# Message-passing layer on one core: node table first, radial pieces made inside the message loop, three one-hot buffers

## What is computed

```
s_j   = (silu(x[src][:, 384:] @ W1 + b1)) @ W3 + b3          # depends on the node alone
rbf   = sqrt(2/R) * sin(n * pi * r / R) / r,  n = 1..20      # radial functions of an edge
basis = rbf * cutoff(r) @ W2 + b2                            # 20 -> 384
s1, s2, s3 = split(s_j * basis)
msg   = [ v_j * s1 + s3 * edge_vector , s2 ]
x1    = x + segment_sum(msg, dst)
h     = silu([norm(vUV), s] @ Wu1 + bu1) @ Wu2 + bu2         # of x1, by node; gives a second message by source
x2    = x1 + segment_sum(second message of src, dst)
y     = layernorm(x + x2)
```

## Time and profile before

| | us |
|---|---|
| median of 3 runs | 714.84 (711.1 to 719.67) |
| profiled execution, its span from first to last instruction | 711.8 |
| first gather of the loop (L486) | 144.38 |
| last product of the loop (L929) | 550.55 |
| PE busy in the span | 505.8 (71%) |
| DVE busy | 537.0 (75%) |
| ACT busy | 389.5 (55%) |
| POOL busy | 370.2 (52%) |

### The profile page before, as it was taken

The page is one execution under the profiler, slowest core; times in us unless marked ns, Lnnn a source line. Parts: engine busy times, 40 slices in busy tenths (PEclk is TensorE's granted clock), DMA queues, the critical chain, the costliest instruction groups (busy, mean ns, idle before and its releaser), DMA issues.

```text
span 711.8 us, 13058 instructions
## 1 busy us (share of the span) xinstructions
PE 505.8 (71%) x4260; PEld 234.1 (33%) x4269; DVE 537.0 (75%) x1192; ACT 389.5 (55%) x713; POOL 370.2 (52%) x375
## 2 busy tenths in 40 slices
PE   0276430038888888888888888888888286689996
PEld 0232110013333333334433333333333153344443
DVE  8868861029999999999999999999999443354283
ACT  1054331046777777776776777777776364343200
POOL 5004440067777777777777777777773131025300
PEclk9975555559999999999999999999999688689999
DMA  8413777699888888898888888888884400000021
GB/s 277 166 21 99 199 229 222 183 256 306 269 269 272 269 275 270 267 275 268 269 273 269 270 271 271 270 270 269 273 271 149 160 3 0 1 0 1 2 89 56
DMA packets 54193, 139.26 MB, mean 196 GB/s; under 512 B 10366, under 2 KB 21850, under 8 KB 54124
## 3 DMA queue, kind: packets, MB, share of 16 engines
q0 software_dynamic: 25120, 102.91, 46.3%
q1 hardware_dynamic: 23132, 25.80, 12.8%
q10 hardware_dynamic: 5872, 9.68, 4.1%
HBM read 120.47 MB, written 17.54 MB: 194 GB/s over the span
## 4 chain that ended last, share of the span: by engine, by line
DVE 39%; PE 35%; DMA 8%; issue 8%; ACT 3%; SPq 2%; POOL 2%; DVEq 1%; ACTq 1%; POOLq 0%
PE psum L1192 11%; DVE side L929 10%; PE psum L1282 9%; DVE hot L920 5%; DMA part_rows<-side 5%; DVE side L926 4%; PE psum L1157 4%; DVE work L929 3%; DVE work L947 3%; PE psum L1186 3%; PE psum L1251 3%; DVE hot L911 2%; SPq L358 2%; DVE side L916 2%; DMA side<-node_table,src_c 2%
## 5 line engine op out<-in xcount | busy, mean ns | idle before, releaser
L486 POOL DMA_INDIRECT side<-node_table,src_c x234 | 224.4, 959 | 71.3 <-issue 60.4
L604 ACT ACTIVATE side<-key_no,less_key 128x320 bf16<-128x320 f32 x314 | 159.3, 557 | 30.7 <-SPq L384 28.9
L612 ACT ACTIVATE side<-side,one_f 128x640 bf16<-128x640 bf16 x157 | 128.1, 816 | 10.0 <-PE psum L1168 10.0
L1157 PE MATMUL psum<-w2s,radial 123*128 123x384 bf16 x314 | 78.7, 333 | 66.3 <-DVE side L929 43.5
L1186 PE MATMUL psum<-side,hot 128*32 128x512 f32 x468 | 123.1, 605 | 0.5 <-DVE side L929 0.5
L929 DVE TENSOR_TENSOR side<-side,psum 128x768 f32<-128x768 f32 x117 | 110.5, 945 | 0.0
L486 POOL DMA_INDIRECT work<-node_table,src_c x80 | 76.8, 960 | 60.6 <-SPq L384 36.5
L1192 PE MATMUL psum<-side,hot 128*32 128x128 f32 x1404 | 99.4, 277 | 0.0
L926 DVE TENSOR_TENSOR side<-side,psum 128x512 f32<-128x512 f32 x117 | 79.4, 678 | 1.3 <-DMA side<-node_table,src_c 1.3
L1168 PE MATMUL psum<-side 128*128 128x320 bf16 x314 | 70.3, 306 | 0.5 <-ACT side L612 0.5
L1192 PEld LDWEIGHTS psum<-side,hot 128*32 128x32 f32 x1404 | 68.0, 109 | 0.1
(11 more groups left out here) (202 smaller groups left out, 738.0 us busy)
## 6 DMA issues: line engine op xcount, KB each, us to landing
radial<-part_rows SPq DMA_DIRECT2D x36, 270.0 KB
part_rows<-side SPq DMA_DIRECT2D x6, 810.0 KB, 12.7
side<-node_table,src_c POOLq DMA_INDIRECT x234, 4.2
sum_rows<-stage SPq DMA_DIRECT2D x212, 16.0 KB
node_table<-work ACTq DMA_DIRECT2D x10, 320.0 KB, 7.6
sum_rows<-zeros_bf SPq DMA_DIRECT2D x1, 2688.0 KB, 18.8
side<-sum_rows ACTq DMA_DIRECT2D x10, 256.0 KB, 4.7
xw<-in_x ACTq DMA_DIRECT2D x1, 2304.0 KB
```

The lines of the kernel that those rows point to most:

```text
L486: g.indirect_dma_start(out=rows[i % SLOT_PAIRS][:, j, :], out_offset=None, in_=node_table, in_offset=bass.IndirectOffsetOnAxis(ap=src_c[:, ...
L604: a.activation(key_off[:, b, j, :], key_no[:, :], ACT.Abs, bias=less_key[:, t:t + 1]).then_inc(L["key_off_made"], 1)
L612: a.activation(key_hot[:, b, :, :], key_off[:, b, :, :], ACT.Relu, bias=one_f[:, :], scale=-1.0).then_inc(L["key_hot_made"], 1)
L1157: last = mm(bank[2 * (i % 2) + j][:, 0:C3], radial[0:RROWS + 3, t * P:(t + 1) * P], w2s[:, :], start=True, stop=True)
```

## The change

1. **Node table first.** ACT loads x's s part, W1, b1, W3 and x's vector part into a buffer of their own (`x_in`) ahead of all else, and the zeroing of `sum_rows` goes to its queue. DVE interleaves the ten table multiplies with the edge tables; the table has four buffers (TABLES) and three PSUM banks (FILTER_BANKS), and the multiply reads the filter in PSUM. Casts and edge attribute copies go to ACT, the splits of W2, the constants and the zeroing of the counts to GpSimd.
2. **Radial pieces in the loop.** PIECES is 9, of 768 columns. r and the coefficient are stored as f32 and loaded by broadcast on 120 partitions (`load_r`, `load_coef`), with no pick matrix and no `spread`. Piece 0 is made before the loop, piece i (1 to 8) in it, from pair `piece_at(i)` on, which is 0 for piece 1 and 18(i-1)-8 for the others; its first edges are used at pair 18i. DVE's steps stand behind pairs 0, 1 and 4 of the piece, ACT's (`sine`, `high_part`, `middle_part`) at its steps 3, 5 and 7, GpSimd's two subtractions behind its gathers 13 and 15. `part` and `wave` have one buffer and lie in `xw`; `load_stack` copies from chip memory to chip memory without `part_rows`. SP's steps of a piece (six stack copies, then the rows of the next piece) stand behind the sum store number `stores_before(i)`.
3. **No barrier at the first pass.** The first pass is straight code without `pass_begin`; further passes, if any edge needs them, stand in an `If`. Each engine waits for what it needs itself.
4. **Three one-hot buffers** (HOTS = 3).
5. x is loaded again into `xw` in front of the last three sum stores, and Wu2 goes into W3's tile.

```diff
-HOTS = 2
+HOTS = 3
-PIECES = 6
-PB = 3
+PIECES = 9
+FILTER_BANKS = 3
+TABLES = 4
...
+        def piece_at(i):
+            return 0 if i == 1 else PIECE_PAIRS * (i - 1) - 8
+        def piece_pairs(step):
+            return {piece_at(i) + step: i for i in range(1, PIECES)}
+        def stores_before(i):
+            return -(-(piece_at(i) + 2) // GP)
...
+            def load_r(i):
+                if i:
+                    sp.wait_ge(S["turn_begun"], i)
+                sp.dma_start(r_in, rc_piece(0, i)).then_inc(S["r_loaded"], 16)
+            def load_coef(i):
+                if i:
+                    sp.wait_ge(S["wave_scaled"], i)
+                sp.dma_start(coef_in, rc_piece(1, i)).then_inc(S["coef_loaded"], 16)
             def load_stack(i):
-                sp.wait_ge(parts_stored[i % 2], 16 * (i // 2 + 1))
+                sp.wait_ge(S["lo_made"], i + 1)
                 for q, k in enumerate(STACK):
...
-                                 part_rows[k].rearrange("(n c) f -> n c f", c=CHUNKS)[:, :, i * PC:(i + 1) * PC]
-                                 ).then_inc(stack_in[i], 16)
+                                 part[:, k, :]).then_inc(stack_in[i], 16)
...
+                    if n in pieces:
+                        load_stack(pieces[n])
+                        if pieces[n] + 1 < PIECES:
+                            load_r(pieces[n] + 1)
+                            load_coef(pieces[n] + 1)
+                    if pieces and n == NG - 4:
+                        load_x()
...
+            for b in range(TABLES):
+                pool.wait_ge(table_stored[b], 16 * through(NW, b, TABLES))
...
+            less_high_at, low_at = piece_pairs(SLOT_PAIRS + 5), piece_pairs(SLOT_PAIRS + 7)
+            for i in range(PAIRS):
+                gather(i)
+                if i in less_high_at:
+                    less_high(less_high_at[i])
+                if i in low_at:
+                    low_part(low_at[i])
...
+            def high_part(i):
+                act.wait_ge(S["wave_scaled"], i + 1)
+                if i:
+                    act.wait_ge(stack_in[i - 1], 16 * PARTS)
+                a.copy(part[:, 0, :], wave).then_inc(S["hi_made"], 1)
+            def middle_part(i):
                 act.wait_ge(S["wave_less_hi"], i + 1)
+                a.copy(part[:, 1, :], wave).then_inc(S["mid_made"], 1)
...
+            sine_at, high_at, middle_at = piece_pairs(3), piece_pairs(5), piece_pairs(7)
+            def key_pass(first):
                 for i in range(PAIRS + 1):
                     if i < PAIRS:
                         key_offsets(i)
                     if i:
                         key_hots(i - 1)
+                    if first and i in sine_at:
+                        sine(sine_at[i])
+                    if first and i in high_at:
+                        high_part(high_at[i])
+                    if first and i in middle_at:
+                        middle_part(middle_at[i])
                     if i >= GP + 2 and (i - GP - 2) % GP == 0:
                         take_sums((i - GP - 2) // GP)
...
+            turns_at, remainder_at, scaled_at = piece_pairs(0), piece_pairs(1), piece_pairs(4)
+            def piece_steps(i):
+                if i in turns_at:
+                    turns(turns_at[i])
+                if i in remainder_at:
+                    remainder(remainder_at[i])
+                if i in scaled_at:
+                    scaled(scaled_at[i])
```

More of the change, by code:

```diff
@@ new lines, in _, with gather @@
+            pool.wait_ge(S["edges_turned"], 5)
+            pool.wait_ge(S["span_made"], 2)
+            pool.wait_ge(S["r_stored"], 16)
+            pool.wait_ge(S["coef_stored"], 16)
+            words = NW * TCOL // 2
+            g.memset(work[:, 0:words], 0.0).then_inc(S["counts_zeroed"], 1)
+            def gather(i):
+                if i >= SLOT_PAIRS:
+                    pool.wait_ge(L["summed"], i - SLOT_PAIRS + 1)
+                for j in range(2):
+                    g.indirect_dma_start(
+                        out=rows[i % SLOT_PAIRS][:, j, :], out_offset=None, in_=node_table,
+                        in_offset=bass.IndirectOffsetOnAxis(ap=src_c[:, 2 * i + j:2 * i + j + 1], axis=0)
+                    ).then_inc(gathered[i % SLOT_PAIRS], 16)
@@ L1108, in _ @@
[L1108 to L1114 removed]
+            for w in range(6, NW):
+                filter_of(w)
+            pe.wait_ge(S["attr_taken"], 3)
```

705 lines of the change are left out of this document (344 added, 361 removed).

## The result

The changed kernel takes **800.85 us** (median of 4 runs, 798.73 to 805.67) against 715.21 us (4 runs, 711.10 to 719.67) for the kernel before: a ratio of 1.1193, 95% interval 1.1121 to 1.1264. The forecast was 698 us with a range up to 728. The profiled execution has a span of 803.8 us.

What follows compares the result with a forecast made beforehand. Before: a serial radial round trip, then a loop with VectorE 96% busy, GpSimd and matmul close. 711.8 - 87 (first part) + 69 (loop) + 2 (tail) = 696 profiled, 699 median, said 698; range 662 to 728.

Steps and rivals of the forecast that it cites:

- The first gather: End of the first part: table first and no round trip start gathers at 57 us (50 to 68), gain 87.
- T1: From first gather to end of piece 1's high subtraction: gather 13 and subtraction 35.1 + 1.7, first rows 3; 40 us.
- T2: Same point of piece 2, ten pairs later: 75 us after the first gather, 3 of it for its radial row.
- Stack 0: Radial stack of piece 0, stored chip memory to chip memory, landing 10 us after the first gather, with the first row.
- The transfers of a piece: Stack and row loads in the loop, 10.5 us a piece: late gathers and sum stores add 1.5 us (0 to 5).
- rival 3: Sync queue: eight issues before a sum store stall ScalarE from about 2 us each; at 3 us, 738 us; chance 0.09.
- ScalarE's block: Loop: ScalarE's middle cast waits for GpSimd's high subtraction, stopping matmul and gathers; a piece costs 52 us instead of 45.4.
- Port: Loop: GpSimd's low subtraction can hold VectorE up to 1.6 us a piece, counted as nothing, as VectorE has 5.8 spare.
- GpSimd takes the bound over: Loop, per 18 pairs: GpSimd 48.6 us against VectorE 46.2; a third one-hot buffer gains only 3 us, in the last pairs.
- The rival without block and queue: Loop costs only GpSimd's own time, 48.6 us a piece, without ScalarE blocking: loop +24, 654 us; chance 0.17.
- The clock, rival 2: Loop: matmul's clock falls to 1.2 GHz in stalls, 3 to 6 us a piece, 722 to 746 us; chance 0.12.
- The signs: Forecast wrong if GpSimd never waits, loop clock row under 10, or a piece's transfers move gathers' landing over 10 us.

Runs made afterwards that it cites:

- three edits: The changed kernel with four stage buffers, spread loads and ScalarE's middle cast three pairs later: 711.41 us, 0.9944 of the kernel before.
- the last version: The changed kernel with subtractions on VectorE, spread loads, middle cast at+8, gathers held, two stage buffers, two one-hot buffers: 687.16 us, 0.9590 of the kernel before.

## Why the prediction was wrong, point by point

The first gather, 57 us: 56.09. *Right*, bounds 50 and 68.

The tail, +2 us: from the last product (640.50) to the end 163.3 us, against 160.3 in the kernel before, +3. *Right.*

The loop was forecast at 476 us from the first gather to the last product and took 584.4. By the steps of that sum, with the middle casts of the changed kernel at 111.93, 164.72 and last 557.37 us:

| | forecast | measured |
|---|---|---|
| T1, middle cast of piece 1 | 40 | 55.8 |
| T2, that of piece 2 | 75 | 108.6 |
| six periods, pieces 2 to 8 | 6 x 53.5 | 6 x 65.4 |
| from there to the end | 80 | 83.1 |

*Stack 0.* "Lands about when the first gathered row does, 10 us after the first gather": it landed 31 us after. I had let the first rows wait for the stack and not the stack for the rows. Sixteen gathers are issued in 20 us, and the earlier trace rows and the windows above show engines 0.66 busy with stack loads alone and 0.85 with both. The issues of the stack alone ended at 65.0, and did hardly sooner (63.8) with the gathers held; what the hold took off is the landing behind them, 15.7 us in place of 23.3. The 16 us of T1 are this.

*T2.* Another 18 us. The radius row of piece 2 was priced at 3 us; its request stands behind stack 1, it was asked for at 128.15 and landed 13.8 us later, and VectorE stood 19.64 us for it: the mechanism of the next step.

*The transfers of a piece, +1.5 us.* **This is the step that failed**, by about 7.5 us a piece. I weighed the queue as issues (rival 3: "from about 2 us an issue on"); the issues took 0.76 to 1.7 us, so by that condition the rival wasn't the case at all. What decides is how long the bytes in front take to drain: 1.8 MB, which I had at 10.5 us alone, took 33 us from the first issue to the landing of the store behind them (175.0 to 207.7), about three times that. And I put no wait on it, as I had counted three groups of cover for ScalarE. The code gives two, 13.4 us here (175.00 to 188.4), of which the issues in front took 9.5. With the loads spread the same bytes cost 7.5 us a piece less.

*ScalarE's block, 52 us a piece in place of 48.6.* Right in place, count and sign: waits of 4.8 to 7.4 us at the eight casts. Its price, 3.4 us, was small: the later cast takes off 5.2 with the loads spread (57.2 to 52.0), and 2.5 in the changed kernel (64.7 to 62.2). With the queue out of the way the period was 57.2 us against my 53.5. That and the 52.0 are both over the forecast by about 3.5 us, which is what 36 gathers take more at 1.05 us each than at the 0.95 that I had.

*Port.* Counted at nothing, bounds 0 and 1.6 us a piece. In the changed kernel 3 of 16 subtractions on GpSimd held an instruction of VectorE. With the stalls gone 14 of 16 did, for 1.2 to 2.1 us each, two a piece: more than the bound, though GpSimd's own row already accounts for the period there.

*GpSimd takes the bound over, and the third one-hot buffer is worth almost nothing*: the first is right only once the two stalls are gone, and the second was measured only with the subtractions on VectorE. The rival without block and queue, 48.6 a piece, would be 51.8.

*The clock, rival 2.* It did fall, from 1.00 to 0.85 in the loop, and right behind the stall that ends at 207.8 us pairs of matmuls of L1218 take 1.07 us, up to 213 us, and 0.62 from 215 us on; the granted clock is 0.50 from 208.2 to 213 us and 1.00 from 215 to 220. An estimate from these rows: some 5 us of matmul at half speed cost at most 2.5 us of a piece, and these would be part of what the queue costs. The clock rises as edits remove the stalls, to 0.94 with three and 0.99 in the last version, and no run has the stalls without it or it without the stalls. So it goes with the stalls, and its own share of the 65.4 us stays open. The Trainium skill's page TensorE: Matmul & The Clock Gate (section "HAM oscillation — how this bites in real kernels") was weighed in the forecast, and by it the clock falls in every repeated wait; the 0.85 agree with it, and the row at 28 to 36 us, from which I argued against it, was no fair witness for stalls of 14 us.

*The signs.* Of those that were to show the forecast wrong two came: the clock row is under 10 in the loop, and while the transfers of a piece are in flight gathers land late. Those issued from 175 to 208 us took 13.5 us at the median, against 4.2 in the kernel before. Little hangs on them: VectorE waited 20.7 us in all for gathered rows from 100 to 650 us.

*The chances.* First part and tail hold, and the block is where it was forecast. Of the 108 us that the loop is over, 16 are stack 0, 18 the row of piece 2, and 71 the six periods, about 45 of them by the queue and 22 by the longer gathers. The first two and the 45 are transfers that came late. The rival that came true had 0.09, because its condition asked the wrong quantity.

## What to carry to other kernels

A store on which a loop waits must not stand behind bulk loads in the same queue: work out how many bytes are in front of it, at the rate that the other traffic leaves, and set that against the cover that the number of buffers gives, counted in the code. Work that is put inside a tight loop wants its place on each engine's order checked against the pace of the others, and small pieces of it spread; when VectorE and GpSimd are both near the bound, as here, work moved from one to the other shows in the period of the loop. And an issue of transfers belongs to an engine for which nobody waits.

## What was not expected of the hardware

A sum store of 4 x 16 KB landed after 17 to 22 us behind 1.8 MB in its own queue, and after 7.1 at most when the same 1.8 MB were in another. Gathers, in GpSimd's queue, landed in 5.7 us at the median and 14.2 at most in the changed kernel (4.2 and 10.1 in the kernel before). GpSimd's gather instruction itself grew from 0.959 us to 1.05 on average: most take 0.95 as before, some 1.5. The cause stays open. It isn't the load of the DMA engines, which were 0.86 busy in the loop of the kernel before, 0.76 in the changed kernel and 0.90 with three edits; and in the changed kernel the gathers within 30 us behind a load of a piece took 1.04 us, the others 1.05. And one chip ran the kernel before in 807 us and not 715, with the same mean clock (0.896 and 0.890), which is why each ratio here is to runs of its own job.
